# Attention and mixture-of-experts on one core: identity products at the start, norm and shift exchanged, an earlier turn of chunk 1, four banks for the shared downs

## The chip, the cores and the metric

One core of a Trainium2 chip runs the whole program in one launch. The metric is the device time of an execution in microseconds (us). PE is the matrix engine (TensorE), DVE the vector engine, ACT the scalar engine, POOL is GpSimd and SP is the queue that issues most transfers.

## The reference

x has 2048 rows of 512 float32 values. The result is two blocks, each with a residual and a layernorm:

```
qkv = x @ w_qkv                        16 heads of 32
q, k = unit_norm(q), unit_norm(k)
q, k = rope(q), rope(k)                even heads only
a = softmax(causal(q @ k.T * q_gain)) @ v @ w_out
x = layernorm(x + a)
scores = softmax(x @ gate_w);  top 2 of 8 experts (hidden 352)
routed = sum of weight * (silu(x @ w_gate[e]) * (x @ w_up[e])) @ w_down[e]
shared = (silu(x @ sw_gate) * (x @ sw_up)) @ sw_down          hidden 704
out = layernorm(x + routed + shared)
```

## The kernel before, in words

**Precision.** Most large products are made of two-part operands: a high part in a rounded 32-bit form (fp32r) and a low part (raw minus high). ACT makes the high part, DVE the low part, and PE adds high x high, low x high and high x low. The products with the softmax weights, and the turns, take plain float32 operands.

**Attention.** The 16 heads go in 4 groups of 4 (g = 0 to 3). In a group the 2048 rows are 4 chunks of 512. The score blocks of a group are 40 slots (`STEP_AT`: chunk 0 has slots 0 to 3, chunk 1 slots 4 to 11, chunk 2 slots 12 to 23, chunk 3 slots 24 to 39; `ORDER` says which 128 keys a slot takes). Every engine runs the same list of slots, each with its own instructions, and semaphores join them. PE does at each slot the scores (`pe_scores`, L1529), then work that tables attach to that slot, then the values of the slot before (`pe_values`, L1576 for the column sums by ones, L1579 for the values, `pe_sums` L1588). At slot 0 of group 1 to 3 the values are those of slot 39 of the group before. A slot in `HELD` puts the values off by one slot, slot 1 among them.

**Tables.** `PROJECT_AT` says at which slot a tile of 128 rows is projected (`pe_project`, L1482; 12 products of 384 columns), `NORMALISE_AT` and `ROTATE_AT` where DVE norms and rotates a chunk (`dve_norms` L1759 to L1766, `dve_rotate` L1775 to L1792; POOL rotates k), `TURN_AT` where q (part 0) or k (part 1) of a chunk is turned, `STACK_AT` where SP loads the turned copy. Negative entries are slots of the group before: chunk 1 of the next group has its last two projections at slots 36 and 37, its norms at 36 and its rotation at 37. Group 0 has its own tables (`..._FIRST`), which the change does not touch.

**A turn.** `pe_turn` (L1499) makes four 128 x 128 transposes into bank 3 (`turn_ps`) once the chunk is rotated. ACT writes the high part (`act_turn_high`, L1658), DVE the low part (`dve_turn_low`, L1797). SP stores both to DRAM (`store_turned`, L1398 and L1400), waits until they have landed (L1413), and loads them in another arrangement (`stack`, L1415) into `q_stack` or `k_stack`, three transfers of 256 KB. The scores of chunk 1 wait for `q_stack` at slot 4 and for their own keys of `k_stack` at the first diagonal block, slot 7.

**Order within a slot.** SP: stores of turned parts, stacks, then the store of a chunk's output. The output of chunk 3 is stored by SP after slot 39 and before slot 0 of the next group (L1421). DVE: low parts of turns first, then the outputs of the last chunk (`dve_outputs`, L1817 to L1829), the rotation, the key sums, the norms. ACT: exponentials (L1683), the copy of the output (L1667), copies of projections (L1637 to L1644), high parts of turns. In group 1 to 3 PE does projections ahead of turns at the same slot.

**The opening.** PE waits for the identity (`consts_ready`), then runs `OPENING`: nine projections and the two turns of chunk 0. A projection of tile n waits for the high and low part of tile n of x, the first one also for the high part of the weights (L1728) and, ahead of its last four products, for their low part (L1732). `OPENING_HIGH` is ACT's order, `OPENING_LOW` that of DVE: x low parts (L1723), weights, the exponents' shift (`dve_shift`, L1833 to L1842, five small instructions), norms and rotations of chunks 0 and 1.

**The shared downs.** `pe_shared_down` (L739) makes one output tile of 128 rows in bank n % 2, and DVE adds it to the residual (L1124, L1132). n counts 0 to 15 in the first half of the shared expert, 16 to 31 in the second. PE takes tile n when DVE has read tile n - 2. Banks 2 and 3 hold the router's counts and logits, which DVE reads up to `place_int` (L1226, the 24th router step).

Of the kernel before, what the change touches and what calls it, by code (L numbers as in the profile page):

```python
# [32 lines left out]
ALU = mybir.AluOpType  # L33
# [3 lines left out]
P = 128  # L37
# [6 lines left out]
NC, TPC = T // CH, CH // P  # L44
# [15 lines left out]
              (2, 0): 1, (2, 1): 2, (2, 2): 3, (2, 3): 5, (3, 0): 8, (3, 1): 9, (3, 2): 10, (3, 3): 11}  # L60
NORMALISE_AT = {(0, 0): -12, (1, 0): -4, (2, 0): 4, (3, 0): 11}
ROTATE_AT = {(0, 0): -11, (1, 0): -3, (2, 0): 6, (3, 0): 13}
TURN_AT = {(0, 0): -8, (0, 1): -5, (1, 0): 1, (1, 1): 3, (2, 0): 8, (2, 1): 13, (3, 0): 16, (3, 1): 23}
STACK_AT = {(0, 0): -4, (0, 1): -2, (1, 0): 2, (1, 1): 4, (2, 0): 10, (2, 1): 15, (3, 0): 16, (3, 1): 31}


PROJECT_FIRST = {(2, 1): 0, (2, 2): 1, (2, 3): 3, (3, 0): 8, (3, 1): 9, (3, 2): 10, (3, 3): 11}
# [18 lines left out]
MASK_BY_PRODUCT = {7, 20, 21, 22, 38, 39}  # L86

EARLY = 2 * TPC + 1
LATE_X_AT = {1: [12], 2: [13], 3: [14], 5: [15]}
X_UNITS = [[0], [1], [2], [3]] + [[t, t + 1] for t in range(TPC, NT, 2)]  # L90
OPENING = [("p", n) for n in range(9)] + [("t", 0), ("t", 1)]
OPENING_HIGH = [("x", 0), ("x", 1), ("x", 2), ("p", 0), ("x", 3), ("p", 1), ("x", 4), ("x", 5), ("p", 2), ("x", 6), ("x", 7),
                ("p", 3), ("p", 4), ("x", 8), ("p", 5), ("x", 9), ("p", 6), ("x", 10), ("p", 7), ("x", 11),
                ("t", 0), ("t", 1), ("p", 8)]
OPENING_LOW = [("x", 0), ("w", 0), ("x", 1), ("x", 2), ("x", 3), ("x", 4), ("x", 5), ("x", 6), ("x", 7), ("shift", 0), ("norm", 0),
               ("x", 8), ("rotate", 0), ("norm", 1), ("x", 9), ("t", 1), ("rotate", 1), ("x", 10), ("x", 11)]
FILL_AT = [7, 9, 10, 12, 13, 14, 20, 21, 22, 23, 25, 28, 30]


# [54 lines left out]
def build(nc, x, x_across, w_qkv, w_out, q_gain, gate_w, w_gate, w_up, w_down, sw_gate, sw_up, sw_down,  # L154
          rope_cos, rope_sin, numbers, out):
    with ExitStack() as ctx:
# [40 lines left out]
        ident = at("ident", 209408, [P, P], F32)  # L197
# [5 lines left out]
        shift = at("shift", 210176, [P, HEADS // 2], F32)  # L203
# [9 lines left out]
        y_ps, sums_ps, qkv_ps, turn_ps = bank  # L213
# [233 lines left out]
        def shared_down(half, slot, low, hc):  # L447

            if half == 1 and (low, hc) == (1, 2):
                return spill[:]  # L450
            first = (DOWN_0, DOWN_1)[half] + (low * 3 + hc) * D
            return ffn_w[:, slot, first:first + D]
# [224 lines left out]
        def pe_shared(pe, half):  # L677
# [4 lines left out]
            for c in range(NC + 1):  # L682
                for hc, (p0, p1) in enumerate(shared_chunks(half)):
# [36 lines left out]
                    if hc == 0 and c == NC:  # L720
# [4 lines left out]
                        for tt in range(2, TPC):  # L725
                            pe_shared_down(pe, half, slot, c - 1, tt, range(3))

        def pe_shared_down(pe, half, slot, c, tt, parts):

            b = half * NC + c  # L730
            n = NC * b + tt
            if parts[0] == 0 and n >= 2:
                pe.wait_ge(down_read, n - 1)
            pe.wait_ge(hid_high, 3 * b + parts[-1] + 1)
            pe.wait_ge(hid_low, 3 * b + parts[-1] + 1)
            for k in parts:
                both = half == 0 and k == 2
                for hs, low in ((hid_h, 0), (hid_h, 1)) if both else ((hid_h, 0), (hid_l, 0), (hid_h, 1)):
                    mm = nc.tensor.matmul(bank[n % 2][:], hs[:, k, tt * P:(tt + 1) * P], shared_down(half, slot, low, k),  # L739
                                          start=(k == 0 and hs is hid_h and low == 0), stop=(k == 2 and low == 1))  # L740
            if parts[-1] == 2:
                mm.then_inc(down_done, 1)
# [330 lines left out]
        def dve_shared(dve, half):  # L1073
            for c in range(NC):
# [34 lines left out]
                for tt in range(TPC):  # L1109
# [11 lines left out]
                    if half == 0 and t < STASHED:  # L1121
                        if n >= 2:
                            dve.wait_ge(half_stored[n % 2], 16 * (n // 2))
                        nc.vector.tensor_tensor(stage[:, n % 2], bank[n % 2][:], x1[:, t], ALU.add).then_inc(down_read, 1)  # L1124
                    else:
                        if half == 0 and tt == 0:
                            wait_scattered(dve, c)
                        if half == 1 and t == 0:
                            dve.wait_ge(half_loaded, 16 * STASHED)
                        if half == 1 and extras_first(t):  # L1130
                            dve.wait_ge(extras_added, TOPK * (t + 1))
                        nc.vector.tensor_tensor(x1[:, t], bank[n % 2][:], x1[:, t], ALU.add).then_inc(down_read, 1)  # L1132
                        if half == 1 and c == NC - 1:
                            dve.wait_ge(down_read, n + 1)
                            nc.vector.bn_stats(stats[:, tt], x1[:, t]).then_inc(ln_steps, 1)
                            if tt >= TPC - 2:
                                last_deviations(dve, tt)
# [454 lines left out]
        @block.tensor  # L1592
        def _(pe):
            pe.wait_ge(consts_ready, 1)
            for kind, n in OPENING:
                if kind == "p":
                    pe_project(0, n // TPC, n % TPC)
                else:
                    pe_turn(0, n // 2, n % 2)
# [19 lines left out]
        def squares_of(g, c):  # L1619

            return (squares, squares_second, squares_third, squares)[c] if not later(g) else squares
# [133 lines left out]
        def dve_norms(g, c, inside=None):  # L1755

            C = NC * g + c
            nc.vector.wait_ge(qkv_copied, 4 * (C + 1))
            nc.vector.tensor_reduce(sq_sum[:], squares_of(g, c)[:], AX, ALU.add).then_inc(norm_steps, 1)  # L1759
            nc.vector.wait_ge(norm_steps, 13 * C + 1)  # L1760
            nc.vector.tensor_scalar(sq_sum[:], sq_sum[:], UNIT_EPS, None, ALU.add).then_inc(norm_steps, 1)
# [195 lines left out]
```

## Time and profile before

| | us |
|---|---|
| median of 3 runs | 1038.64 (1038.08 to 1041.03) |
| the profiled execution's own time | 1034.4 |
| its span | 1032.7 |
| PE busy in the span | 999.6 (97%) |
| DVE, ACT, POOL busy | 651.0, 547.3, 376.6 |

The profiled execution is one execution; its time is 4.2 us below the median of the runs, and 1.7 us of it lie outside the span. In the timeline a line is a merged run of instructions: start, length from the first start to the last end, engine, source line, operation, operands, count, and in brackets the idle time of that engine before it with what ended it. Ends of matrix products overlap the next start.

### The profile page before, as it was taken

To read this page: it belongs to the slowest core of one execution; us is meant where nothing else is said; L and a number is where in the kernel's file an instruction comes from. 1 tells how busy PE (TensorE), PEld (TensorE's weight loads), DVE (VectorE), ACT (ScalarE), POOL (GpSimd) and SP (SyncE) were. 2 spreads that over 40 slices of the span, in tenths; PEclk is the share of its full clock that TensorE was granted. 3 is DMA by queue.
4 is the path that set the end of the run, shared out by engine and by line. 5 is a ranking of instruction groups with operands and counts; after the bars stand their busy time and mean duration, and the time that the engine had idled before them with its cause. 6 is when DMAs were issued, how large, how long until landed. Compare 5 with 4: busy or idle time off the path is not lost.

```text
span 1032.7 us, 17543 instructions
## 1 busy us (share of the span) xinstructions
PE 999.6 (97%) x5951; PEld 724.4 (70%) x5951; DVE 651.0 (63%) x1138; ACT 547.3 (53%) x906; POOL 376.6 (36%) x312
## 2 busy tenths in 40 slices
PE   6899999999999999999999999999999999999996
PEld 7564566646666455664367778889999999998885
DVE  5699584896849968398679666444334333324776
ACT  4778776687767867668846632223333333321213
POOL 0332132321323312131534107563475666424431
PEclk9999999999999999999999999999999999999998
DMA  6447333473342723418146206593455553414433
GB/s 205 129 117 213 95 103 97 108 215 92 102 132 84 224 73 102 123 52 252 44 129 188 78 31 229 191 289 120 156 166 166 166 168 116 145 53 126 135 110 123
DMA packets 115821, 140.60 MB, mean 136 GB/s; under 512 B 10272, under 2 KB 74016, under 8 KB 115744
## 3 DMA queue, kind: packets, MB, share of 16 engines
q1 hardware_dynamic: 83552, 102.56, 33.4%
q10 hardware_dynamic: 27072, 20.20, 6.2%
q0 software_dynamic: 5120, 16.78, 5.0%
q8 instruction: 52, 0.85, 0.4%
q14 instruction: 25, 0.20, 0.1%
HBM read 83.93 MB, written 55.57 MB: 135 GB/s over the span
## 4 chain that ended last, share of the span: by engine, by line
PE 77%; DVE 10%; ACT 6%; DMA 2%; POOL 2%; issue 2%; SPq 0%; DVEq 0%; ACTq 0%
PE scores L634 15%; PE scores L1529 10%; PE bank L1482 10%; PE scores L694 8%; PE bank L1579 8%; PE bank L622 8%; PE bank L739 5%; PE scores L542 4%; ACT probs L1683 4%; DVE key_sum L1808 4%; PE bank L1576 3%; DVE x L1164 1%; PE scores L602 1%; POOL wqkv_l L1886 1%; PE bank L1588 1%
## 5 line engine op out<-in xcount | busy, mean ns | idle before, releaser
L1683 ACT ACTIVATE probs<-scores,shift_now 128x1024 f32<-128x1024 f32 (+3 forms) x296 | 273.5, 978 | 74.1 <-PE scores L1529 48.8
L1808 DVE TENSOR_TENSOR key_sum<-key_sum,probs 128x2048 f32<-128x2048 f32 (+1 forms) x96 | 205.3, 2138 | 50.7 <-PE bank L1579 19.1
L1529 PEld LDWEIGHTS scores<-q_stack,k_stack 96*128 96x128 f32 x624 | 99.2, 188 | 121.6 <-ACT probs L1683 66.1
L1529 PE MATMUL scores<-q_stack,k_stack 96*128 96x512 f32 (+3 forms) x624 | 177.1, 396 | 6.6 <-ACT probs L1683 2.8
L1579 PE MATMUL bank<-probs,v_sb 128*32 128x512 f32 (+3 forms) x1184 | 135.8, 533 | 0.0
L634 PE MATMUL scores<-ffn_w,xt_h 128*128 (+1 forms) x608 | 125.1, 328 | 0.0
L1044 DVE TENSOR_TENSOR ht_l<-scores,ht_h 128x256 fp32r<-128x256 f32 x39 | 16.6, 425 | 142.2 <-ACT ht_h L827 142.2
L634 PEld LDWEIGHTS scores<-ffn_w,xt_h 128*128 128x128 f32 x608 | 101.0, 189 | 3.5
L1263 POOL TENSOR_TENSOR ffn_w<-raw,ones 128x1408 fp32r<-128x1408 f32 (+4 forms) x32 | 64.1, 2014 | 97.6 <-PE bank L622 78.7
L1558 POOL TENSOR_SCALAR_AFFINE_SELECT probs<-probs 128x512 f32<-128x512 f32 x40 | 44.3, 1115 | 136.4 <-ACT probs L1683 136.4
L694 PE MATMUL scores<-x1T_h,ffn_w 128*128 128x512 f32 x352 | 89.5, 391 | 0.0
L1267 POOL TENSOR_TENSOR ffn_w<-raw,ffn_w 128x1408 fp32r<-128x1408 f32 (+3 forms) x31 | 80.3, 2600 | 1.9
L694 PEld LDWEIGHTS scores<-x1T_h,ffn_w 128*128 128x128 f32 x352 | 65.7, 188 | 13.5
L881 ACT CAST hid_h<-silu 128x512 fp32r<-128x512 f32 (+1 forms) x24 | 14.9, 620 | 105.7 <-DVE silu L1080 105.7
L622 PE MATMUL bank<-ffn_w,ht_h 128*128 (+2 forms) x234 | 67.6, 397 | 0.7 <-issue 0.7
L1579 PEld LDWEIGHTS bank<-probs,v_sb 128*32 128x32 f32 x1184 | 29.7, 109 | 47.0 <-issue 39.3
L634 PE MATMUL scores<-ffn_w,xt_l 128*128 (+1 forms) x304 | 61.0, 322 | 0.0
L834 ACT COPY y_tile<-bank 128x512 f32<-128x512 f32 x39 | 22.9, 587 | 69.3 <-PE bank L622 58.9
L1786 POOL TENSOR_TENSOR rope_prod<-qk_even,sin 128x128 f32<-128x128 f32 x8 | 4.5, 557 | 142.9 <-DVE qk_even L1775 142.9
L739 PE MATMUL bank<-ffn_w,hid_h 128*128 128x512 f32 x176 | 54.8, 394 | 1.4 <-DVE x L1132 1.1
L1327 POOL DMA_INDIRECT extra<-y_sorted,place_int x32 | 32.3, 1008 | 55.8 <-DMA y_sorted<-y_tile 20.9
L1482 PE MATMUL bank<-wqkv_h,xT_h 128*128 128x384 f32 x232 | 51.4, 343 | 0.9 <-DVE xT_l L1723 0.7
(254 smaller groups left out, 1760.2 us busy)
## 6 DMA issues: line engine op xcount, KB each, us to landing
k_stack<-turn_scratch SPq DMA_DIRECT2D x48, 256.0 KB, 4.3
q_stack<-turn_scratch SPq DMA_DIRECT2D x45, 256.0 KB, 3.9
x_sorted<-zeros SPq DMA_DIRECT2D x39, 256.0 KB, 3.5
y_sorted<-y_tile ACTq DMA_DIRECT2D x39, 256.0 KB, 2.9
x_tile<-x_sorted ACTq DMA_DIRECT2D x148, 64.0 KB, 2.0
turn_scratch<-turned_h SPq DMA_DIRECT2D x31, 256.0 KB, 2.1
turn_scratch<-turned_l SPq DMA_DIRECT2D x31, 256.0 KB, 2.3
raw<-w_gate SPq DMA_DIRECT2D x8, 704.0 KB, 5.2
```

The lines of the kernel that those rows point to most:

```text
L622: mm = nc.tensor.matmul(out_tile[:], hs[0:kn, k, :], moving(slots[j - 1], DOWN + (low * 3 + k) * D, D, kn), start=(m == 0 and k == 0), sto ...
L634: mm = nc.tensor.matmul(to[:, 0:FH], xs[:, k, :], moving(slot, first + (low * KC + k) * FH, FH), start=(m == 0 and k == 0), stop=(m == 2 a ...
L694: mm = nc.tensor.matmul(scores[:, which, n % 2, :], stationary(half, slot, which, low, k, hc), xs[:, k, c * CH:(c + 1) * CH], start=(m == ...
L739: mm = nc.tensor.matmul(bank[n % 2][:], hs[:, k, tt * P:(tt + 1) * P], shared_down(half, slot, low, k), start=(k == 0 and hs is hid_h and ...
L1263: last = nc.gpsimd.tensor_tensor(high, src, one, ALU.mult)
L1267: last = nc.gpsimd.tensor_tensor(low, src, high.bitcast(F32), ALU.subtract)
L1482: mm = nc.tensor.matmul(qkv_bank(n)[:, 0:3 * P], xs[:, k, tok], ws[:, k, :], start=(m == 0 and k == 0), stop=(m == 2 and k == KC - 1))
L1529: mm = nc.tensor.matmul(scores[:, p, hh, lo:CH], k_stack[0:3 * HD, h, j * P:(j + 1) * P], q_stack[0:3 * HD, i % 2, h, lo:CH], start=True, ...
L1558: nc.gpsimd.affine_select(out=block, in_=block, compare_op=ALU.is_ge, fill=0.0, base=0, pattern=[[0, HG], [1, P]], channel_multiplier=-1). ...
L1579: mm = nc.tensor.matmul(y_ps[HD * h:HD * (h + 1), lo:CH], v_sb[:, j, HD * h:HD * (h + 1)], exponents(g, slot)[:, h, lo:CH], start=(slot == ...
L1683: nc.scalar.activation(exponents(g, slot)[:, 2 * p:2 * p + 2, lo:CH], scores[:, p, :, lo:CH], ACT.Exp, bias=shift_now[:, p:p + 1]).then_in ...
L1808: nc.vector.tensor_tensor(key_sum[:, :, lo:CH], key_sum[:, :, lo:CH], probs[:, slot % 4, :, lo:CH], ALU.add).then_inc(sum_dve, 1)
```

## The change

It has five parts. (1) After `consts_ready` PE makes 12 plain float32 products of the identity with itself (128 x 128) into bank 3, whose result nothing reads. (2) In `OPENING` the turns of chunk 0 come ahead of the ninth projection; in `OPENING_LOW` the shift moves from before chunk 0's norms to after its rotation, and the low part of x tile 8 from before the rotation to after it. (3) `dve_norms` of the first chunk waits for the tables itself (the gains). (4) For groups 1 to 3 the turns of chunk 1 move from slots 1 and 3 to slots 0 and 2, their stacks from slots 2 and 4 to slots 1 and 3. (5) From the fifth down product on, four banks are used in place of two, with one new wait of PE for 24 router steps.

```diff
-TURN_AT = {(0, 0): -8, (0, 1): -5, (1, 0): 1, (1, 1): 3, (2, 0): 8, (2, 1): 13, (3, 0): 16, (3, 1): 23}
-STACK_AT = {(0, 0): -4, (0, 1): -2, (1, 0): 2, (1, 1): 4, (2, 0): 10, (2, 1): 15, (3, 0): 16, (3, 1): 31}
+TURN_AT = {(0, 0): -8, (0, 1): -5, (1, 0): 0, (1, 1): 2, (2, 0): 8, (2, 1): 13, (3, 0): 16, (3, 1): 23}
+STACK_AT = {(0, 0): -4, (0, 1): -2, (1, 0): 1, (1, 1): 3, (2, 0): 10, (2, 1): 15, (3, 0): 16, (3, 1): 31}
...
+WARM_UP = 12
...
-OPENING = [("p", n) for n in range(9)] + [("t", 0), ("t", 1)]
+OPENING = [("p", n) for n in range(8)] + [("t", 0), ("t", 1), ("p", 8)]
...
-... ("x", 7), ("shift", 0), ("norm", 0),
-               ("x", 8), ("rotate", 0), ("norm", 1), ("x", 9), ("t", 1), ("rotate", 1), ("x", 10), ("x", 11)]
+... ("x", 7), ("norm", 0),
+               ("rotate", 0), ("x", 8), ("shift", 0), ("norm", 1), ("x", 9), ("t", 1), ("rotate", 1), ("x", 10), ("x", 11)]
...
+        def down_bank(n):
+            return bank[n % (2 if n < TPC else 4)]
...
+            if parts[0] == 0 and n == TPC:
+                pe.wait_ge(router_steps, PLACE_STEPS)
             if parts[0] == 0 and n >= 2:
-                pe.wait_ge(down_read, n - 1)
+                pe.wait_ge(down_read, n - 1 if n < TPC + 2 else max(TPC, n - 3))
...
             pe.wait_ge(consts_ready, 1)
+            for _ in range(WARM_UP):
+                nc.tensor.matmul(turn_ps[:, 0:P], ident[:], ident[:], start=True, stop=True)
...
             nc.vector.wait_ge(qkv_copied, 4 * (C + 1))
+            if C == 0:
+                nc.vector.wait_ge(tables_loaded, 48)
```

## Rows read from the trace of the kernel before

**Rows 1.** Page, part 1: busy time, share of the span, instructions.

```profile
PE 999.6 (97%) x5951; PEld 724.4 (70%) x5951; DVE 651.0 (63%) x1138; ACT 547.3 (53%) x906; POOL 376.6 (36%) x312
```

**Rows 2.** Timeline of the opening (POOL, PE), and line L1499's weight loads.

```profile
1.89 0.29 POOL L1900 TENSOR_SCALAR_AFFINE_SELECT ident<-ident 128x128 f32<-128x128 f32 x1 [0.24 <-POOL ones L1898]
...
7.75 1.62 PE L1482 MATMUL scores<-wqkv_h,xT_h 128*128 128x384 f32 x4 [7.75 <-DVE wqkv_h L1728]
...
10.45 1.48 PE L1482 MATMUL scores<-wqkv_l,xT_h 128*128 128x384 f32 x4
...
12.95 0.86 PE L1482 MATMUL scores<-wqkv_h,xT_l 128*128 128x384 f32 x4
...
28.90 0.60 PE L1499 MATMUL bank<-ident,qk_even 128*128 128x128 f32 x4
...
L1499 PEld LDWEIGHTS bank<-ident,qk_even x64: 138/140/143, 28.7 to 461.0; 128*128 128x128 f32 x64
```

**Rows 3.** Timeline of the opening, DVE, and PE's wait at its end.

```profile
7.68 1.76 DVE L1732 TENSOR_TENSOR wqkv_l<-wqkv_raw,wqkv_h 128x1536 fp32r<-128x1536 f32 x1
...
17.98 1.29 DVE L1723 TENSOR_TENSOR xT_l<-xT_raw,xT_h 128x512 fp32r<-128x512 f32 x2 [0.79 <-ACT xT_h L1625]
19.20 0.17 DVE L1833 TENSOR_SCALAR gain_abs<-gain 128x16 f32<-128x16 f32 x1
...
20.09 1.21 DVE L1759 TENSOR_REDUCE sq_sum<-squares 128x32 f32<-128x1024 f32 x1
...
28.27 1.20 DVE L1759 TENSOR_REDUCE sq_sum<-squares_second 128x32 f32<-128x1024 f32 x1
...
38.09 0.93 PE L1482 MATMUL bank<-wqkv_h,xT_h 128*128 128x384 f32 x4 [0.30 <-DVE xT_l L1723]
```

**Rows 4.** Timeline from group 0 into group 1, the instructions around chunk 1's turns.

```profile
152.88 1.22 DVE L1759 TENSOR_REDUCE sq_sum<-squares 128x32 f32<-128x1024 f32 x1 [2.10 <-ACT v_sb L1644]
...
158.40 1.07 PE L1588 MATMUL bank<-key_sum,ones 128*32 128x512 f32 x8
...
160.37 0.28 DVE L1792 TENSOR_TENSOR qk_odd<-qk_odd,rope_prod 128x128 f32<-128x128 f32 x1
...
162.34 0.79 DVE L1829 TENSOR_TENSOR y_norm<-y_norm,inv_sum 128x512 f32<-128x512 f32 x1
...
162.75 0.60 PE L1499 MATMUL bank<-ident,qk_odd 128*128 128x128 f32 x4
...
163.82 0.65 PEld L1482 LDWEIGHTS bank<-wqkv_h,xT_h 128*128 128x128 f32 x4 [0.21 <-ACT v_sb L1644]
...
165.01 0.32 SPq L1400 DMA_DIRECT2D turn_scratch<-turned_l  x1
...
172.27 0.76 PEld L1529 LDWEIGHTS scores<-q_stack,k_stack 96*128 96x128 f32 x4 [0.16 <-DMA q_stack<-turn_scratch]
...
183.62 0.50 PE L1529 MATMUL scores<-q_stack,k_stack 96*128 96x256 f32 x2 [1.45 <-DMA k_stack<-turn_scratch]
```

**Rows 5.** Group 3: timeline, then windows (length, PE busy, PEclk, DMA share, GB/s).

```profile
428.22 1.19 PE L1529 MATMUL scores<-q_stack,k_stack 96*128 96x512 f32 x4 [2.16 <-DMA q_stack<-turn_scratch]
...
428.00:430.00 2.00, 1.78 (x18) 0.82 0.62 235
430.00:432.00 2.00, 2.00 (x21) 0.50 0.57 161
432.00:434.00 2.00, 2.00 (x13) 0.82 1.03 229
```

**Rows 6.** Stores of turned low parts (L1400), and a DMA queue between 418 and 423.

```profile
DMA to landing us min/median/max: 2.0/2.3/5.0
...
q8 instruction: 1, 0.02, 2.3%
```

**Rows 7.** Timeline of DVE at L1226, and the page's group of down products.

```profile
619.72 0.18 DVE L1226 CAST place_int<-place_float 128x32 int32<-128x32 f32 x1
...
L739 PE MATMUL bank<-ffn_w,hid_h 128*128 128x512 f32 x176 | 54.8, 394 | 1.4 <-DVE x L1132 1.1
```

More of the change, by code:

```diff
@@ L94 @@
                 ("t", 0), ("t", 1), ("p", 8)]
-OPENING_LOW = [("x", 0), ("w", 0), ("x", 1), ("x", 2), ("x", 3), ("x", 4), ("x", 5), ("x", 6), ("x", 7), ("shift", 0), ("norm", 0),
-               ("x", 8), ("rotate", 0), ("norm", 1), ("x", 9), ("t", 1), ("rotate", 1), ("x", 10), ("x", 11)]
+OPENING_LOW = [("x", 0), ("w", 0), ("x", 1), ("x", 2), ("x", 3), ("x", 4), ("x", 5), ("x", 6), ("x", 7), ("norm", 0),
+               ("rotate", 0), ("x", 8), ("shift", 0), ("norm", 1), ("x", 9), ("t", 1), ("rotate", 1), ("x", 10), ("x", 11)]
 FILL_AT = [7, 9, 10, 12, 13, 14, 20, 21, 22, 23, 25, 28, 30]
@@ L738, in pe_shared_down @@
                 for hs, low in ((hid_h, 0), (hid_h, 1)) if both else ((hid_h, 0), (hid_l, 0), (hid_h, 1)):
-                    mm = nc.tensor.matmul(bank[n % 2][:], hs[:, k, tt * P:(tt + 1) * P], shared_down(half, slot, low, k),
+                    mm = nc.tensor.matmul(down_bank(n)[:], hs[:, k, tt * P:(tt + 1) * P], shared_down(half, slot, low, k),
                                           start=(k == 0 and hs is hid_h and low == 0), stop=(k == 2 and low == 1))
@@ L1123, in dve_shared @@
                             dve.wait_ge(half_stored[n % 2], 16 * (n // 2))
-                        nc.vector.tensor_tensor(stage[:, n % 2], bank[n % 2][:], x1[:, t], ALU.add).then_inc(down_read, 1)
+                        nc.vector.tensor_tensor(stage[:, n % 2], down_bank(n)[:], x1[:, t], ALU.add).then_inc(down_read, 1)
                     else:
@@ L1131, in dve_shared @@
                             dve.wait_ge(extras_added, TOPK * (t + 1))
-                        nc.vector.tensor_tensor(x1[:, t], bank[n % 2][:], x1[:, t], ALU.add).then_inc(down_read, 1)
+                        nc.vector.tensor_tensor(x1[:, t], down_bank(n)[:], x1[:, t], ALU.add).then_inc(down_read, 1)
                         if half == 1 and c == NC - 1:
```

## The prediction

> **What bounds the kernel now.** I read the page's busy shares first: PE is busy 97% of the span and no other engine above 63% [rows 1]. A change can therefore gain only what PE idles or runs slowly, about 33 us in all, and any new wait of PE is paid in full unless an idle stretch follows that takes it up. I then listed PE's idle stretches over 0.15 us in the timeline. They are the wait for the first weights; gaps in the opening, where DVE is the longest chain; two waits for stacked q or k in groups 1 and 3 [rows 4, 5]; and four short ones at the downs [rows 7]. The windows show the granted clock below 1.00 in one place before the last 10 us, right after the longer stack wait [rows 5]. Last I read the stretch from slot 37 of group 0 to slot 7 of group 1, instruction by instruction, because the moved turns land there.
>
> **Identity products.** PE starts projecting at 7.75 and its first 16 products take until 12.95; the other 92 of the nine projections take until 28.90, 0.173 us each [rows 2]. At that pace 16 take 2.8, so the slow start costs 5.2 - 2.8 = 2.4 us. The slow ones stand 0.32 apart, which is 384 columns at the 1.2 GHz level, the others near the 2.4 GHz level. The identity is ready at 2.2 [rows 2], so PE can work 5.5 us earlier, and the twelve products hold nothing up if they end before 7.75. No row shows them. The lower bound is a third of a slow 384-column product each, 12 x 0.107 = 1.3 us, after which PE would idle and the clock might stay low. The upper bound takes two instructions each, as plain float32 products have elsewhere here, at twice the 0.14 us of a weight load at full clock [rows 2]: 24 x 0.28 = 6.7 us, to 8.9 at worst, less once the clock rises. The clock rose some 5 us after PE's first work, so I take a rise near 6 to 7 and an end near 7.5. Then the first eight products end at 9.14 and the next four wait for the low weights, done at 9.44 [rows 3]: 0.3 of the 2.4 stays, and 2.1 us is the gain.
>
> **Opening order.** The next limit is DVE, which runs from 17.98 almost without a gap until PE waits for its low part of x at 38.09 [rows 3]. The norms of chunk 0 now start at 20.09, after the low parts end at 19.27 and the shift (19.20 to 20.09, 0.9 us). With the faster start the low parts end at 17.2; with about 0.2 for ACT's copy of the fourth projection (an estimate) the norms start at 17.4. From these norms to those of chunk 1 it is 28.27 - 20.09 = 8.2 us and the shift's 0.9 now lies in that stretch: 26.5 against 28.27. The opening gains **1.8 us**. Without the clock's rise it is 19.5 + 8.2 + 0.9 = 28.6, a loss of 0.3: the shift was half hidden where it stood. The ninth projection behind the turns fills PE's wait for ACT's copy and is bound by the same DVE chain; nothing more for it. The added wait for the tables costs nothing, since the shift used them at 19.20 already and their loads are long issued.
>
> **Chunk 1 turned a slot sooner.** The turn of q needs DVE's rotation, which ends at 160.65 in group 1 [rows 4]. That chain cannot start sooner: DVE idled 2.10 us for ACT's copy of the last projection before its norms at 152.88, and none of this is moved. PE has finished the scores of slot 0 at 158.40 [rows 4] and used to do slot 39's values, slot 1's scores and a projection before the turn at 162.75. Placed at slot 0, the turn makes PE stand from 158.40 to 160.68: **2.28 us**. All that waits behind it (values, scores of slot 1) is late too. The turn's 0.4 us also used to fill PE's wait for ACT's copy of the projection, of which 0.21 was left [rows 4]; that wait grows by 0.4. Each group pays 2.7, three groups **8.1 us**. Below nothing is excluded: no later idle stretch of PE takes it up.
>
> What it buys: at slot 4, q was 0.1 late in group 1 and 2.16 in group 3 [rows 4, 5]. Does q come sooner? The turn starts 2.1 sooner, but now slot 39's values (about 1.4), two copies of ACT (1.2), DVE's low part (0.7) and, ahead of its store on SP, the output of chunk 3 (DVE outputs 160.65 to 163.13, 2.5) [rows 4] come before it: by these estimates the low store is issued at 167.9 against 165.01, 2.9 later, for a slot 4 that is 2.7 later. With a wait of 0.1 before, q is 0.3 late each time: **0.8 us** more; bounds 0 and 1.5. k gains real room: its turn at slot 2 has no such work ahead, so the 1.45 of group 1 goes [rows 4]. In group 3 the 2.16 goes and so does the clock's dip, (2 x 0.18) + (2 x 0.50) + (2 x 0.18) = 1.7 us [rows 5], if no store is late. In sum **-5.3**.
>
> Both waits came with a late store: median 2.3 us to landing, the longest 5.0, and beside that in group 3 stands one packet of an instruction queue [rows 6]. Group 2, with its stores at 2.0, has no wait. So they are hits on a marginal schedule, not its rule. One hit costs q the wait beyond its slack, 2.1. One q store in three was late before; I take one in three again: **+2.1** (bounds 0 and 6.3). The Trainium skill, Runtime: NRT & Kernel Launch, section Instruction fetch mechanics, has each engine fetch its program in blocks, hidden behind execution. By it no such hit would be due to fetching, and 2.1 would be left out; the row shows a fetch beside the late store but not that it was the cause.
>
> **Clock after the new stalls.** A wait of 2.16 was followed by 0.50 [rows 5]; one of 1.45 was not. 2.28 lies just beyond the first, followed by transposes and narrow products; bounds 0 and 3 x 1.7 = 5.1. I take one drop, **+1.7**: the nearest row fell, but by a hair's breadth of length only. The Trainium skill, TensorE: Matmul & The Clock Gate, section Why this matters for your kernels, allows longer idle gaps than these before the clock falls. By it these three cost nothing and the sum would be 1.7 lower; the drop after 2.16 speaks against it.
>
> **Downs.** PE waited 1.1 us for DVE's reads [rows 7]; the third and fourth bank remove that: **-1.1**, bounds 0 and -1.4. The new wait for the router costs nothing: its last step is written by 619.9 [rows 7], and PE reaches the fifth tile only after a whole further chunk of gate and up products, which cover it; were it not met, the downs of chunk 1 and all behind them would wait for DVE. Without the read to wait for, PE meets DVE next at the low part of the hidden values, behind the same gate and up products.
>
> **Sum** against the profiled execution (1034.4): -1.8 + 8.1 + 0.8 - 5.3 - 1.1 + 2.1 + 1.7 = +4.5, so 1038.9. The runs' median is 4.2 above that execution; against it 1038.6 + 4.5 = **1043.1**.
>
> **Rivals.**
> - The clock stays high after the new stalls, since products lie close on both sides of each: +2.8, 1041.4. For it, the 1.45 us wait without a drop; against it, the drop after 2.16 [rows 4, 5]. This is what the Trainium skill's clock page, named above, would have. It counts as no change: 0.3% (3.1 us) is about what a measurement of this kernel can tell from none.
> - Cancelled: the clock stays and no q store is late either, as in group 2: +0.7, 1039.3. Against it, that the stores still share the queues with everything they share now.
> - Faster: the runs' 4.2 us over the profiled execution are a further late q with its dip (2.2 + 1.7 = 3.9) in groups that the profile shows without, and the earlier turn leaves none. That is +0.7 - 3.9, and up to 0.9 more if DVE's chain in the opening follows the clock whole: 1034.6. It decides only if two such hits go and none comes; against it, q is no sooner at slot 4.
> - The identity products do not keep the clock up (too short or idle behind them): the opening loses 0.3 in place of gaining 1.8: 1045.2.
> - Every new stall is followed by the low clock and q is late more than once: +4.5 + 3.4 + 2.1 = 1048.6.
>
> **Chances.** The forecast 0.33, no rise 0.13, every stall 0.16, all slower; clock stays 0.14 and cancelled 0.12, both no change; faster 0.12. So slower 0.62, same 0.26, faster 0.12. The range from 1037.5 to 1049.0 leaves out most of the faster case and the far end of the bounds (+0.7 + 5.1 + 6.3). The likeliest side alone runs from 1041.8 to 1049.0.
>
> **What would show it.** Right: the first projection's products 0.17 apart; PE idle 2.3 before L1499 near slot 0 of groups 1 to 3, released by DVE L1792; the store of the turned q on SP behind the output's; no wait for `k_stack`; no L739 idle for L1132. Wrong: PE without idle at slot 0, or q landed well ahead of slot 4. Windows of the granted clock after each stall settle the third term.

## The result, and the profile after

The changed kernel takes 1044.28 us (median of 10 runs, 1041.45 to 1048.19), the kernel before in the same job 1037.85 (1034.58 to 1041.03). The ratio is 1.0059 with a 95% interval of [1.0043, 1.0075]: about 6 us slower. Its profiled execution took 1041.45 us with a span of 1039.7. A second job with the same kernel, told below, gave 1.0038 [1.0024, 1.0052], about 4 us slower; the forecast was 4.5.

Page of the changed kernel, part 1, then PE's own list of waits (engine and waiting line, what ended the wait: us in total, times, longest):

```profile
PE 1000.4 (96%) x5975; PEld 726.7 (70%) x5975; DVE 652.2 (63%) x1138; ACT 548.1 (53%) x906; POOL 375.2 (36%) x312
...
PE bank L1506 <- DVE qk_odd L1803: 7.7, 4, 2.2
...
PE scores L1536 <- DMA q_stack<-turn_scratch: 2.8, 4, 1.0
PE bank L746 <- DVE hid_l L1093: 2.3, 1, 2.3
...
PE bank L1489 <- ACT v_sb L1653: 1.5, 3, 0.5
```

PE runs 24 instructions more, the products, which take 5.49 us; its busy time grows by only 0.8 [rows 1], because the first projections are faster and the low clock of group 3 is gone. The span grew by 7.0. By the last store of the attention's output it is 4.0 (534.82 against 530.82); the rest comes later. The first line of the list is the price: PE waits for DVE's rotation four times, once in the opening (1.1, where before has 1.0) and three times in slot 0. The waits for k's stack and for the reads of the downs are gone from the list. The stack of q now makes PE wait at chunk 1's first scores in each of groups 1 to 3, and once more, by 0.28, later in group 2. The new wait for the router steps ends no idle stretch of PE.

Timeline of the opening, PE and DVE (answers to [rows 2, 3]):

```profile
2.22 5.49 PE L1603 MATMUL bank<-ident 128*128 128x128 f32 x24 [2.22 <-POOL ident L1911]
7.46 1.21 PE L1489 MATMUL scores<-wqkv_h,xT_h 128*128 128x384 f32 x4
8.50 0.86 PE L1489 MATMUL scores<-wqkv_h,xT_l 128*128 128x384 f32 x4
...
17.35 1.22 DVE L1770 TENSOR_REDUCE sq_sum<-squares 128x32 f32<-128x1024 f32 x1 [0.27 <-ACT v_sb L1653]
...
25.05 0.94 DVE L1732 TENSOR_TENSOR xT_l<-xT_raw,xT_h 128x512 fp32r<-128x512 f32 x1
...
25.41 0.90 POOL L1803 TENSOR_TENSOR qk_even<-qk_even,rope_prod 128x128 f32<-128x128 f32 x1
25.92 0.42 DVE L1844 TENSOR_SCALAR gain_abs<-gain 128x16 f32<-128x16 f32 x1
...
27.08 1.21 DVE L1770 TENSOR_REDUCE sq_sum<-squares_second 128x32 f32<-128x1024 f32 x1
...
36.91 0.93 PE L1489 MATMUL bank<-wqkv_h,xT_h 128*128 128x384 f32 x4 [0.29 <-DVE xT_l L1732]
```

The products run from 2.22 to 7.71, the first projection starts at 7.46 without a wait, and from 8.50 on the projections stand 0.17 to 0.20 apart, where the first sixteen of before stood 0.32 apart. Chunk 0's norms start at 17.35 (forecast 17.4), chunk 1's at 27.08 (forecast 26.5). The missing 0.5 lies between them: the low part of x took 0.94 instead of 0.69 and the first instruction of the shift 0.42 instead of 0.17. Both run beside POOL's last instruction of k's rotation, which took 0.90 instead of 0.47. PE passes the end of the opening at 36.91 instead of 38.09 [rows 3].

Timeline of group 0 into group 1, and the same places of groups 2 and 3 (answers to [rows 4, 5]):

```profile
159.14 0.28 DVE L1803 TENSOR_TENSOR qk_odd<-qk_odd,rope_prod 128x128 f32<-128x128 f32 x1
159.47 0.66 PE L1506 MATMUL bank<-ident,qk_odd 128*128 128x128 f32 x4 [2.21 <-DVE qk_odd L1803]
...
165.23 0.97 PE L1489 MATMUL bank<-wqkv_h,xT_h 128*128 128x384 f32 x4 [0.51 <-ACT v_sb L1653]
165.84 0.34 SPq L1428 DMA_DIRECT2D y_scratch<-y_norm  x1
166.22 0.43 SPq L1405 DMA_DIRECT2D turn_scratch<-turned_h  x1
166.70 0.45 SPq L1407 DMA_DIRECT2D turn_scratch<-turned_l  x1
...
174.47 1.20 PE L1536 MATMUL scores<-q_stack,k_stack 96*128 96x512 f32 x4 [0.73 <-DMA q_stack<-turn_scratch]
...
288.78 0.66 PE L1506 MATMUL bank<-ident,qk_odd 128*128 128x128 f32 x4 [2.21 <-DVE qk_odd L1803]
...
304.02 1.20 PE L1536 MATMUL scores<-q_stack,k_stack 96*128 96x512 f32 x4 [0.98 <-DMA q_stack<-turn_scratch]
...
418.88 0.66 PE L1506 MATMUL bank<-ident,qk_odd 128*128 128x128 f32 x4 [2.21 <-DVE qk_odd L1803]
...
433.92 1.19 PE L1536 MATMUL scores<-q_stack,k_stack 96*128 96x512 f32 x4 [0.79 <-DMA q_stack<-turn_scratch]
```

The rotation ends at 159.42 and the turn starts at 159.47, after 2.21 us of idle PE; the projection behind waits another 0.51 for ACT's copy; the turned low part leaves SP at 166.70, behind the output's store, 1.7 later than before, and takes 2.65 us to land where it took 2.0. So q is 0.7 to 1.0 late. No window between 12 and 1020 us has a granted clock below 1.00 in this execution.

One thing in this profile was in no forecast. Timeline of PE and DVE at the downs of the routed half:

```profile
664.59 0.84 PE L746 MATMUL bank<-ffn_w,hid_h 128*128 128x512 f32 x3
...
670.75 0.69 DVE L1139 TENSOR_TENSOR x<-bank,x 128x512 f32<-128x512 f32 x1 [6.38 <-remote]
...
677.40 0.47 PE L746 MATMUL bank<-ffn_w,hid_h 128*128 128x512 f32 x1 [2.30 <-DVE hid_l L1093]
```

PE issued the last products of the tile by 665.3, but DVE, which waits for their count, starts 5 us later. PE then waits 1.21 (at 672.08, just as DVE's next instruction, L1087, ends; the profile itself puts this one down to issue) and 2.30. The profile of before has nothing like it. More on it below.

### The profile page after: what moved, and what is told of

It is laid out like the page before. It is cut to its first block, busy times and chain, and to the rows that moved or that the text cites. A ratio compares the mean times of both kernels' runs of the same rounds, so it can differ in the third digit from the quotient of the medians.

```text
span 1039.7 us, 17592 instructions
## 1 busy us (share of the span) xinstructions
PE 1000.4 (96%) x5975; PEld 726.7 (70%) x5975; DVE 652.2 (63%) x1138; ACT 548.1 (53%) x906; POOL 375.2 (36%) x312
## 4 chain that ended last, share of the span: by engine, by line
PE 73%; DVE 11%; ACT 6%; DMA 4%; POOL 2%; issue 2%; SPq 1%; another core or an unknown queue 1%; DVEq 0%; ACTq 0%; POOLq 0%
PE scores L635 14%; PE scores L695 11%; PE scores L1536 9%; PE bank L623 8%; PE bank L1489 8%; PE bank L1586 7%; PE bank L746 6%; ACT probs L1692 4%; DVE key_sum L1819 4%; PE bank L1583 3%; PE scores L543 2%; DMA q_stack<-turn_scratch 2%; PE scores L603 1%; POOL wqkv_l L1897 1%; DMA turn_scratch<-turned_l 1%
## 5 line engine op out<-in xcount | busy, mean ns | idle before, releaser
L1489 PE MATMUL bank<-wqkv_h,xT_h 128*128 128x384 f32 x232 | 51.5, 343 | 3.2 <-DVE xT_l L1732 1.7
```

The costliest lines, as they stand in the source:

```text
L1489: mm = nc.tensor.matmul(qkv_bank(n)[:, 0:3 * P], xs[:, k, tok], ws[:, k, :], start=(m == 0 and k == 0), stop=(m == 2 and k == KC - 1))
```

## Experiments

All run to the end of the same computation. They ran in four further jobs (experiments 1 to 4, 5 to 8, 9 to 11, and 12). Each kernel is compared with runs of the kernel before on the same chip in its job; those medians were 1039.02, 1034.60, 1034.37 and 1032.43 us, so only ratios and differences go across jobs.

**1. Turns and stacks put back.** The changed kernel with the two tables of before.

```
-TURN_AT = {..., (1, 0): 0, (1, 1): 2, ...}
-STACK_AT = {..., (1, 0): 1, (1, 1): 3, ...}
+TURN_AT = {..., (1, 0): 1, (1, 1): 3, ...}
+STACK_AT = {..., (1, 0): 2, (1, 1): 4, ...}
```

> The changed kernel with TURN_AT and STACK_AT of before. My theory, the moved turns cost three stalls of 2.2 us, three lengthened waits for ACT's copy and three waits of about 0.8 us for q: no idle of PE at slot 0 of groups 1 to 3, waits for stacked q or k as before (0 to 2.2 us, at random), and a time 2 to 3 us below before (ratio about 0.998), from the opening (1.2) and the downs (1.1). Rival, the loss lies in the late DVE read of the eleventh down tile near 670 us (over 3 us there): then the time stays within 1 us of the changed kernel, 5 to 7 us above before.

Measured: 1032.23 us, ratio 0.9933 [0.9912, 0.9955]. The rest of the change is worth about 7 us, more than twice what was forecast (2.9). The rival falls: the late count near 665 us is in this profile too (PE waits 3.88 at 665.28), and the kernel is faster all the same. Of the waits for stacked k and q at chunk 1's scores, one of 1.02 for k, in group 2, and one of 0.17 are left.

**2. Turns alone.** The kernel before with the changed two tables and nothing else.

> Before with the moved turns and stacks alone. My theory: PE idle 2.2 us before the turn of q in each of groups 1 to 3, q late by 0.7 to 1.0 each time, no wait for k: 3 x (2.2 + 0.4 + 0.8) = 10 us added, less 0 to 5 for the late stacks of before: 5 to 10 us slower, ratio 1.005 to 1.010. Rival, the DVE read near 670 us: time within 2 us of before.

Measured: 1050.39 us, ratio 1.0096 [1.0070, 1.0122], so +10 us, the upper end of the theory. PE's waits in its profile, and the windows (start:end and length, PE, PEld, DVE, ACT and POOL busy, granted clock, DMA share, GB/s) of the second profile of the changed kernel, which is experiment 10:

```profile
PE bank L1499 <- DVE qk_odd L1792: 7.7, 4, 2.2
PE scores L1529 <- DMA q_stack<-turn_scratch: 4.9, 4, 2.6
```

```profile
160.00:164.00 4.00, 4.00 (x33) 2.49 (x32) 0.12 (x1) 1.22 (x3) 0.97 (x2) 0.59 0.00 0
...
290.00:294.00 4.00, 3.83 (x30) 1.77 (x30) 0.12 (x1) 0.12 (x1) 1.44 (x3) 0.57 0.02 4
```

Both windows begin right behind a wait of 2.2 us in slot 0 (in that profile it ends at 159.71 and 290.18). At 0.59 of the clock a stretch of 4.00 us does 2.36 us of full-speed work: 1.6 us lost, and 1.7 at 0.57. The profile of experiment 2 has such stretches at 163 and 293 us. In its group 3, q is late by 2.64 (at 440.92), the longest wait for a stack in any profile, and no low clock follows: the granted clock is 1.00 from 296 to 685 us. The low store of q took 4.4 us to land there, with a packet of an instruction queue from 431.1 to 432.9; experiment 8 is about this.

**3. No products.** The changed kernel with the twelve products left out.

```
-WARM_UP = 12
+WARM_UP = 0
```

> The changed kernel with no products of the identity. My theory: the first 16 projection products take 5.2 us again, the norms of chunk 0 start near 19.5, PE's wait at the tenth projection ends 2 us later than in the changed kernel (near 38.9 against 36.9), and nothing later differs: 2 us over the changed kernel, 8 over before. Rival, the opening is bound by the loads of x: the wait ends within 0.5 us of the changed kernel's.

Measured: 1045.97 us, ratio 1.0070 [1.0048, 1.0092], +7 us. Timeline of its opening, PE:

```profile
7.62 1.62 PE L1489 MATMUL scores<-wqkv_h,xT_h 128*128 128x384 f32 x4 [7.62 <-DVE wqkv_h L1737]
...
38.58 0.94 PE L1489 MATMUL bank<-wqkv_h,xT_h 128*128 128x384 f32 x4 [0.30 <-DVE xT_l L1732]
```

The projections start at the pace of before again, and the opening ends at 38.58 instead of 36.91: in the opening the products are worth 1.7 us (forecast 2.1 without the limit by DVE), and the new order alone costs 0.5 against before (forecast 0.3; against all four profiles with the old opening, which end it at 37.52 to 38.27, it is 0.3 to 1.1). The time as a whole doesn't show this: 1.0070 against the changed kernel's 1.0059 in another job lies inside both intervals.

The same profile shows a second effect of the products, in group 3 (DMA view from 429 to 433, then PE):

```profile
q8 instruction: 1, 0.02, 1.5%
...
turn_scratch<-turned_l SPq DMA_DIRECT2D x1, 256.0 KB, 3.4
...
438.21 1.18 PE L1536 MATMUL scores<-q_stack,k_stack 96*128 96x512 f32 x4 [1.65 <-DMA q_stack<-turn_scratch]
```

Without the products a packet of an instruction queue starts at 429.3, 7.0 behind the end of the wait in slot 0, and stands beside the stores of q. In the changed kernel it starts at 421.5, 2.6 behind that point, the store takes 2.7 and q is 0.79 late. The two kernels differ by the products alone.

**4. Downs in two banks.** The changed kernel with the downs as before.

```
-            return bank[n % (2 if n < TPC else 4)]
+            return bank[n % 2]
...
-            if parts[0] == 0 and n == TPC:
-                pe.wait_ge(router_steps, PLACE_STEPS)
             if parts[0] == 0 and n >= 2:
-                pe.wait_ge(down_read, n - 1 if n < TPC + 2 else max(TPC, n - 3))
+                pe.wait_ge(down_read, n - 1)
```

> The changed kernel with its downs in two banks. My theory: the four waits of PE for DVE's reads come back (1.1 us) and the time is 1 us over the changed kernel; the late DVE read near 670 us has another cause and may or may not appear. Rival, four banks cause that late read: it is gone here, and the time is 2 to 3 us below the changed kernel's.

Measured: 1045.47 us, ratio 1.0068 [1.0047, 1.0089]. Against the 1.0059 of the changed kernel in another job that is +0.9 of 1000, inside both intervals: inconclusive by itself. The rival falls: with two banks the late count is there too (PE waits 3.73 at 677.92, and the clock is low behind it).

**5. Only k sooner.** q's turn and its stack in slot 1, k's in slot 2.

```
-TURN_AT = {..., (1, 0): 0, (1, 1): 2, ...}
-STACK_AT = {..., (1, 0): 1, (1, 1): 3, ...}
+TURN_AT = {..., (1, 0): 1, (1, 1): 2, ...}
+STACK_AT = {..., (1, 0): 1, (1, 1): 2, ...}
```

> The changed kernel with q's turn back in slot 1 (its stack in slot 1 too) and only k's turn and stack a slot sooner than before (slot 2). Theory (the price lies in the turn of slot 0, which waits 2.2 us for VectorE's rotation, and in what it no longer fills): no such wait here, the waits for k's stack gone too, so 1.5 us or less beside the kernel with all turns put back (1032 us), that is 1030 to 1033 us, 6 us or more below the kernel before. Rival (any turn or stack made sooner pushes SyncE's queue into the next late load): a wait of 1 us or more for q's or k's stack in each of three groups, 1034 to 1038 us.

Measured: 1027.23 us, ratio 0.9936 [0.9919, 0.9953]. PE waits for no stack of chunk 1 in its profile (one wait of 0.17 for a q stack, at 324.57, is left), and no window between 12 and 1012 us is below 1.00. As a ratio it is no better than experiment 1; the absolute number is lower because this chip ran the kernel before in 1034.60 (the theory's absolute figures were set from the other chip). Both versions beat both kernels.

**6. The kernel before, once more.**

> The kernel before, unchanged, for a second profile of it. Its first profiled execution (1034.4 us) lies at the low end of its runs (1034.4 to 1041.3). Theory (that execution was a lucky one: TensorE's counts of finished products arrive late by 3 to 6 us between 650 and 680 us in each profile taken since, changed or not in that part): the second profile shows VectorE or ScalarE waiting 4 us or more for finished products in that stretch, a low clock behind it, and a time of 1037 to 1040 us. Rival (the late counts come from the four banks or from the shifted work): none here, no low clock in that stretch, 1034 to 1036 us.

Measured: 1034.08 us, ratio 0.9994 [0.9984, 1.0003] against its own other runs. No late count near 665: the theory fell for this chip. What did come again is the q store of group 3, below. Here the profiled execution (1034.83) and the median agree; why the first profile of before stands 4.2 below the runs beside it stays open. The opening ends at 37.52 here, 0.6 sooner than in the first profile of the same kernel.

**7. Four banks alone.** The kernel before with the downs in four banks.

> The kernel before with the downs in four banks and nothing else. The waits of the downs for VectorE's reads were 1.1 us in all in the profile of before, so the theory gives 0 to 1.5 us less than before (1037 to 1039 us beside 1038.5). Rival one (the banks are what made the version with all turns put back 7 us faster): 3 to 5 us less. Rival two (late counts of finished products come with four banks): 1 us or more slower.

Measured: 1031.15 us, ratio 0.9972 [0.9957, 0.9988], so -2.9 us. Its profiled span is 1.9 below that of experiment 6, and all of it comes after 975 us. There the profile of experiment 6 has these rows (timeline, PE), and this kernel no idle stretch of PE at all:

```profile
975.56 0.50 PE L739 MATMUL bank<-ffn_w,hid_h 128*128 128x512 f32 x1 [0.38 <-DVE x L1132]
1000.82 0.50 PE L739 MATMUL bank<-ffn_w,hid_h 128*128 128x512 f32 x1 [0.48 <-DVE x L1132]
1020.36 0.50 PE L739 MATMUL bank<-ffn_w,hid_h 128*128 128x512 f32 x1 [0.16 <-DVE x L1132]
```

The three make 1.0. Laid side by side, the same instructions of DVE stand level in both profiles at 972, and 0.7, 1.5 and 1.9 us sooner here behind the first, second and third of them: each is worth 0.3 more than its idle row says. Rival two falls. The interval (-1.2 to -4.4) doesn't decide between the theory and rival one.

**8. The opening alone.** The kernel before with the products and the new order of the opening.

> The kernel before with the products of the identity and the new order of the opening, and nothing else. The profiles give 2.4 us less at 184 us for these two, so the theory says 2 to 4 us less than before (1034.5 to 1036.5 us). Rival (the opening is what made the version with all turns put back 7 us faster, the banks nothing): 6 to 7 us less (1031.5 to 1032.5 us).

Measured: 1029.38 us, ratio 0.9955 [0.9939, 0.9972], so -4.7 us, between the theory and the rival. Group 3 of experiment 6 (kernel before) and of this kernel: SP's queue and PE's wait in the timeline, the windows, and the DMA view of the 4 us around q's stores (of before also its GB/s in 40 slices of 0.1 us from 417 on).

```profile
418.29 0.32 SPq L1400 DMA_DIRECT2D turn_scratch<-turned_l  x1
422.26 1.27 SPq L1415 DMA_DIRECT2D q_stack<-turn_scratch  x3
...
427.44 1.77 PE L1529 MATMUL scores<-q_stack,k_stack 96*128 96x512 f32 x4 [1.81 <-DMA q_stack<-turn_scratch]
...
428.00:432.00 4.00, 4.00 (x35) 1.71 (x34) 0.00 (x0) 2.12 (x2) 0.00 (x0) 0.60 0.58 183
...
GB/s 0 0 102 328 348 410 389 430 389 205 21 0 0 0 512 369 328 369 328 348 287 307 410 369 348 348 348 328 82 0 0 20 0 20 0 20 20 20 20 20
...
q8 instruction: 1, 0.02, 2.6%
...
turn_scratch<-turned_l SPq DMA_DIRECT2D x1, 256.0 KB, 3.9
```

```profile
417.13 0.32 SPq L1405 DMA_DIRECT2D turn_scratch<-turned_l  x1
419.21 1.27 SPq L1420 DMA_DIRECT2D q_stack<-turn_scratch  x3
...
428.00:432.00 4.00, 4.00 (x24) 3.32 (x26) 2.32 (x5) 3.50 (x7) 0.00 (x0) 1.00 0.66 160
...
turn_scratch<-turned_l SPq DMA_DIRECT2D x1, 256.0 KB, 2.0
```

In the kernel before, one packet of an instruction queue (16 KB, from 418.47 to 420.12) runs beside q's low store, the store takes 3.9 us to land instead of 2.0, the load of the stack goes out 4.0 behind it instead of 2.1, PE waits 1.81, and the clock is at 0.60 after that. Besides the stores' own packets nothing else moves in these 4 us. The slices show how the store is held: by 419.9 all but its last packets are through, and these go one at a time (20 GB/s) from 420.1 on, just when the instruction packet ends. That fits a store whose share of one DMA engine stands behind the packet; the trace doesn't name the engine of a packet, so this is argued.

With the products ahead that packet came between 412 and 416, in front of the stores, and none of this happens to q in group 3. All seven profiles with q's turn in its old slot fall in line: the three without the products (before, experiments 6 and 7) have the packet at 418 to 419, the late store, the wait of about 2 us and the low clock; the four with the products (experiments 1, 5, 8 and 12) have the packet at 413 to 414, and no wait for q there, though the work itself stands only 1.2 us earlier. Of the profiles with q's turn moved, the two without the products (experiments 2 and 3) have the packet beside the store again, which takes 4.4 and 3.4 us, and the longest waits for q, 2.64 and 1.65; with the products the store takes 2.7 and q is at most 1.15 late. So most of what the opening gives, it gives 380 us later: against experiment 6 this kernel is 1.2 us ahead at the output's store before these rows (415.28 against 416.44) and 4.5 ahead at the last one (525.52 against 530.06).

The shift isn't all gain. In experiments 1 and 8 another packet (300.3 and 300.6) stands beside k's low store of group 2, which takes 4.0 and 3.7 us, and PE waits 1.02 and 0.89 for k; in the kernel before the k store so hit was that of group 1.

**9. Only q sooner.** The changed kernel with k's turn and stack in slots 3 and 4.

```
-TURN_AT = {..., (1, 1): 2, ...}
-STACK_AT = {..., (1, 1): 3, ...}
+TURN_AT = {..., (1, 1): 3, ...}
+STACK_AT = {..., (1, 1): 4, ...}
```

> The changed kernel with k's turn and stack of the next group back where they were (slots 3 and 4), so that of the four moves only q's turn (slot 0) and stack (slot 1) are left. Theory (the turn in slot 0 carries the price: 2.2 us of waiting, a wait for ScalarE's copy that it no longer fills, a late store of q, and falls of the clock behind): as slow as the changed kernel, within 2 us of it, three waits of 2.1 to 2.3 us in slot 0. Rival (k's sooner turn carries part of it, by crowding SyncE's queue and VectorE in slots 2 and 3): 3 us or more faster than the changed kernel.

Measured: 1038.66 us, ratio 1.0037 [1.0020, 1.0055]. The changed kernel in the same job has 1.0038: as far as the intervals tell, the whole price is q's.

**10. The changed kernel, once more.**

> The changed kernel, unchanged, for a second profile and for its time in the same job as the others. It stood 6 us over the kernel before in its own runs, but the parts tried alone (opening -4.7, banks -2.8 us) and the turns alone (+10 us, on another chip) would sum to +2.5 us. Theory (parts add up only if the falls of the clock and the late counts of finished products are told apart from them): 3 to 7 us over the kernel before; three waits of 2.2 us in slot 0; at least one fall of the clock in about half of its runs; no count of a finished product late by over 3 us if the kernel before has none in this job. Rival (the late counts are the changed kernel's own): late again in its profile.

Measured: 1037.27 us, ratio 1.0038 [1.0024, 1.0052]. Three waits of 2.21 to 2.22 us in slot 0, q late by 0.37, 0.76 and 1.15, a low clock behind two of the three waits (the windows under experiment 2), no late count near 665. Six of its runs have a mean clock of 0.997 or 0.998 and take 1036.5 to 1037.3 us; four have 0.992 to 0.994 and take 1039.3 to 1040.9.

**11. The rotation a slot sooner too.** The changed kernel with the last two projections, norms and rotation of the next group's first chunk a slot earlier.

```
-PROJECT_AT = {..., (1, 2): -4, (1, 3): -3,
+PROJECT_AT = {..., (1, 2): -5, (1, 3): -4,
-NORMALISE_AT = {(0, 0): -12, (1, 0): -4, ...}
-ROTATE_AT = {(0, 0): -11, (1, 0): -3, ...}
+NORMALISE_AT = {(0, 0): -12, (1, 0): -5, ...}
+ROTATE_AT = {(0, 0): -11, (1, 0): -4, ...}
```

> The changed kernel, but with the last two projections of the next group's first chunk, its norms and its rotation a slot sooner as well (slots -5, -4, -5 and -4 for -4, -3, -4 and -3), so that VectorE has the rotated values ready when TensorE comes to the turn in slot 0. Theory (the wait for the rotation is the price): the 2.2 us waits of slot 0 shrink below 0.5 us and the kernel comes 7 us or more below the changed kernel, to about the time of the one with only k sooner (7 us below before). Rival (the price is the sooner stores and loads, or the unfilled wait of the second projection): waits in slot 0 gone but 3 us or less gained. Third way (VectorE is late in the slots before, so the wait only shrinks to about 1 us): 3 to 5 us gained.

Measured: 1038.28 us, ratio 1.0040 [1.0025, 1.0055]: nothing gained. PE's waits, and the timeline of slot 0 of group 1:

```profile
PE scores L1536 <- ACT probs L1692: 4.7, 22, 0.4
PE bank L1595 <- DVE key_sum L1819: 4.4, 4, 1.3
...
157.47 2.55 DVE L1819 TENSOR_TENSOR key_sum<-key_sum,probs 128x2048 f32<-128x2048 f32 x1
158.16 0.60 PE L1506 MATMUL bank<-ident,qk_odd 128*128 128x128 f32 x4
160.08 1.06 PE L1595 MATMUL bank<-key_sum,ones 128*32 128x512 f32 x8 [1.32 <-DVE key_sum L1819]
160.20 1.11 ACT L1692 ACTIVATE probs<-scores,shift_now 128x1024 f32<-128x1024 f32 x1 [3.18 <-DVE key_sum L1819]
```

The turn now starts without a wait, at 158.16. But DVE did the rotation ahead of the last sum of the exponentials, and PE's next products and ACT's next exponentials stand behind that sum. PE waits 1.3 there in each group instead of 2.2, and for ACT's exponentials six times more, 1.9 us in all. That makes 5.9, against the 6.6 of the three waits of 2.2. Neither the theory nor the third way names this; the rival has the size, not the cause.

**12. The turn ahead of the projection, in its old slot.** The version of experiment 1, with the order of turn and projection swapped in slots 0 to 3, in PE's list and, by the same edit, in ACT's.

```
-                    opening = not later(g) and slot < STEP_AT[1]
+                    opening = slot < STEP_AT[1]
```

> The version with the turns and stacks put back (7 us below the kernel before), but in slots 0 to 3 of every group the turn is issued ahead of that slot's projection, on TensorE and on ScalarE. So q's turn stays in slot 1, where its rotation is long done, and only stops standing between the projections of slots 1 and 2. It tests the forecast's term of 0.4 us per group by itself. Theory: three waits of 0.5 us of the projection in slot 2 for ScalarE's copy, no wait for the rotation, no late q, 1 to 2.5 us slower than the version it starts from, so 4.5 to 6 us below before. Rival (the turn's sooner place matters by itself, through ScalarE's copies ahead of the exponentials): 4 us or more slower than it, 3 us or less below before.

Measured: 1026.70 us, ratio 0.9949 [0.9932, 0.9966], 5.3 us below before, inside the theory's 4.5 to 6. PE's list of waits has the projection's wait for ACT's copy (L1489 <- ACT v_sb L1653) three times, 0.5 each, as in the changed kernel, and no other new one in the attention. Against experiment 1 the ratio is 1.6 of 1000 higher, as forecast, but the intervals overlap; it is the waits that show the term.

## Why the prediction was right, and where its terms were off

The forecast was +4.5 us over the kernel before, from terms of both signs; measured were +6.1 and +3.9. That the sum came out is in part luck: three terms were too small, two of them gains. What the price of slot 0 is and what releases it was right and is shown; which part of the change removes the late store was wrong.

| step | forecast | measured |
|---|---|---|
| opening | -1.8 | -4.7 alone; 1.2 of it in the opening's rows |
| four banks | -1.1 | -2.9 alone; 1.9 between the spans |
| turns (8.1 + 0.8 - 5.3 + 2.1 + 1.7) | +7.4 | +10.0 alone; on top of the rest (1.0038 - 0.9933) x 1036 = +10.9, or +13.1 with 1.0059 |

- **Slot 0.** Forecast 2.28 us each; 2.21 in all three groups, released by the rotation. Right.
- **The turn no longer fills the wait for ACT's copy.** Forecast 0.4 each on top of 0.2 weight load; measured 0.51 of PE, and the idle time of the weight load went from 0.21 to 0.65. Experiment 12 shows it by itself. Right.
- **q late at slot 4.** Forecast 0.3 each and one late store of 2.1, in sum 2.9. Measured 0.73, 0.98 and 0.79 in the first profile, 0.37, 0.76 and 1.15 in the second, 2.3 to 2.5 in sum, with no store late by 2. The size is right, the split was not. The store is issued 1.7 later where the opening stands 1.2 earlier, so 2.9 against the work around it, as forecast; but with the output's store and the high store 0.9 and 0.5 us ahead of it it takes 2.65 to land, not 2.0. That 0.6 was missing from each group. The one hit did not come, because the products had moved the packet; where they are left out it does come (experiments 2 and 3). The 5.0 that the prediction gave for the longest landing is of a store in the opening; the two beside the waits of before took 4.0 (q) and 4.3 (k).
- **Waits of before gone, -5.3.** They did go, but the step that put q's 2.16 and the clock's 1.7 to the turns failed. Experiment 8 takes the wait of 1.8 and the low clock behind it away with no turn moved, and with the turns moved but no products (experiments 2 and 3) q of group 3 is late by 2.64 and 1.65. Of the 5.3 the turns can claim k's 1.45: with its turn sooner k never waits (the changed kernel and experiments 2 to 5, 10 and 11), in its old slot it waits 0.70 to 1.45 in five of seven profiles. The double booking cancels in the whole change: the wait and the clock go once either way.
- **The clock after the new waits.** Forecast one fall in three. The six profiles with waits of 2.2 us in slot 0 have 18 of them, and in 8 cases a window below 0.9 behind: 0, 2, 1, 1, 2 and 2 per profile. The five profiles with neither that wait nor the late q store (experiments 1, 5, 8, 11 and 12) have none before 640 us, though PE waits 1.3 in experiment 11. So 8/18 x 3 x 1.6 = 2.1 us on average, against 1.7. The prediction took the length of the wait for the sign, and the rows don't bear that out: waits of 2.21 are followed by either, the 2.64 of experiment 2 and the 1.65 of experiment 3 by none, the 1.81 of experiment 6 by the low clock. The rivals in which the clock stays or always falls are both out as a rule, though single executions are like each. The rule of the Trainium skill that the prediction named (TensorE: Matmul & The Clock Gate, Why this matters for your kernels) would have it stay each time, and these rows disagree.
- **Opening.** The products do what was worked out, and the DVE chain limits them as worked out: 1.2 against 1.8, because the low part of x and the shift now run beside POOL's last rotation instruction and take 0.5 longer together; no run separates which slows which. The 1.2 is of the two first profiles. Over all, the opening ends at 37.52 to 38.27 without the change and at 36.73 to 37.24 with it. The step that failed is to count only the opening: shifting where the instruction packets fall was worth more than the time saved. The other sentence drawn from the Trainium skill (Runtime: NRT & Kernel Launch, Instruction fetch mechanics), that fetching is hidden behind execution, is about the fetching engine's own wait, and PE shows none of its own around these packets. The prediction read into it that a fetch would delay nothing else, which that section does not state; the rows of experiments 3 and 8 show the delay by way of the store.
- **Banks.** The forecast took 1.1, the waits listed, with 1.4 as its bound; the runs say 2.9 with an interval from 1.2 to 4.4, and the profiles 1.9. The term left out what each wait costs beyond its idle row, 0.3 (experiment 7).
- **The rival in which the run medians of before hide further late stores** has no such store in any profile to stand on. In experiment 6, on another chip, the profile and the median are the same within 1 us; for the first chip no second profile of before was taken, and the 4.2 stay unexplained.

Open: the counts of finished products that reach DVE and ACT 3 to 6 us late between 650 and 680 us. The first profile of the changed kernel and those of experiments 1 to 4 have them, five in all (experiment 2 among them, with before's downs and opening); the eight of the later jobs have none, among them the changed kernel again. They cost PE 3 to 5 us in waits such as the 1.21 and 2.30 above, and in experiments 1 to 4 a low clock follows. No part of the change is common to all five; what causes them was not found. The first profile of before has none, and there is no profile of before beside experiments 1 to 4, so whether its runs had them there is not known, and the ratios of the changed kernel and of experiments 1 to 4 may hold a part of them.

Open too: the place of the instruction packet was moved only by leaving out all the products. No run tried another number of them.

## What to carry to other kernels

Before work is issued sooner, look up when its operand is ready, on the slowest engine of its chain: a turn placed 2.2 us ahead of its rotation costs those 2.2 us, the filler that it was, and sometimes the clock as well; and pulling the rotation ahead only moves the wait to what it overtakes. When parts of a change meet the same wait, only one can be credited with removing it: test each part alone before adding them. Instructions added anywhere move the later instruction packets, so look at what stands beside them in the DMA view. Here the moves of q's turn lose 10 us or more and the rest wins 7, so the better kernel is the change without them (1032 us where before has 1039).

## What was not expected of the hardware

- A packet of an instruction queue beside a store of 256 KB goes with 3.9 us to landing instead of 2.0, and its place moves with how many instructions stand ahead. The products, 24 more matrix instructions with their weight loads, and a new order at the start moved it from 418.5 to 413.8 us, in front of the store, and took a wait of 1.8 us and a low clock with it. With the products alone left out of the changed kernel, it stands 7.0 instead of 2.6 us behind the turn of slot 0, beside the store again.
- The same wait of 2.2 us, with the same work on both sides, was followed by the lower clock in 8 of 18 cases, and a longer one, of 2.64 us, was not.
- Beside POOL's last rotation instruction, DVE's low part of x and the first instruction of the shift took 0.94 and 0.42 us and POOL's own 0.90; apart from each other they took 0.69, 0.17 [rows 3] and 0.47.
